# Third attention: the masks stored a second time with their halves exchanged, and added by 64-row, 64-column matmuls

## The reference, cut to what matters

```
def _L2_xattn_ref(queries, keys, values, masks, Wq, bq, Wk, bk, Wv, bv, Wo, bo):
    q = (queries @ Wq + bq).reshape(B, S, H, dk).transpose(0, 2, 1, 3)
    k = (keys @ Wk + bk).reshape(B, S, H, dk).transpose(0, 2, 1, 3)
    v = (values @ Wv + bv).reshape(B, S, H, dv).transpose(0, 2, 1, 3)
    scores = jnp.einsum('bhqd,bhkd->bhqk', q, k) / jnp.sqrt(jnp.float32(dk))
    scores = jnp.where(masks[:, None, :, :], scores, jnp.float32(-1000000000.0))
    attn = jax.nn.softmax(scores, axis=-1)
    out = jnp.einsum('bhqk,bhkd->bhqd', attn, v)
...
x = x + jnp.tanh(g_xattn[2]) * _L2_xattn_ref(_layernorm(x, axis=-1), ctx_1024, ctx_1024, mask_BxSxS2_bf1, ...)
```

## Time and profile before

| | us |
|---|---|
| median of three runs | 2752.37 |
| the three runs | 2749.81, 2752.37, 2772.16 |
| the profiled execution, its own time | 2753.38 |
| its span | 2751.6 |
| third attention in the span | about 1428 to 1880 |

### The profile page before, as it was taken

How to read it: one execution, slowest core, us unless ns; L and a number is a source line. 1 busy time by engine, 2 the same in 40 slices (tenths; PEclk the granted TensorE clock), 3 DMA queues, 4 the chain that set the end, 5 groups by cost and what they waited for, 6 DMA issues and landing times. The chain is left out here.

```text
span 2751.6 us, 77920 instructions
## 1 busy us (share of the span) xinstructions
PE 2249.3 (82%) x32227; PEld 1705.9 (62%) x32227; DVE 1791.9 (65%) x4725; ACT 1351.5 (49%) x2507; POOL 1217.9 (44%) x1731
## 2 busy tenths in 40 slices
PE   4999999999959599945648999983888848888597
PEld 3888888887747377734435766662555526666465
DVE  3777777777733488858866766644444458888544
ACT  2555555555513288829964544430111148777332
POOL 1333333434435411127751244445455566777535
PEclk9999999999979799976668988875899967677699
DMA  6112100000035211100000111111444322222263
GB/s 172 58 62 81 66 26 26 25 22 21 18 116 169 65 59 55 48 17 1 1 26 29 33 41 42 41 33 68 135 133 135 108 68 69 81 85 74 82 181 112
DMA packets 212353, 184.49 MB, mean 67 GB/s; under 512 B 33356, under 2 KB 187542, under 8 KB 212000
## 3 DMA queue, kind: packets, MB, share of 16 engines
q1 hardware_dynamic: 192544, 142.51, 17.6%
q0 software_dynamic: 19456, 36.99, 3.8%
HBM read 102.01 MB, written 72.68 MB: 63 GB/s over the span
## 5 line engine op out<-in xcount | busy, mean ns | idle before, releaser
L446 POOL DMA_INDIRECT slots<-row,put x256 | 264.4, 1033 | 251.0 <-issue 100.7
L1777 PE MATMUL experts_H<-experts_xs_t,experts_w 128*128 128x512 f32 x576 | 274.6, 622 | 26.5 <-DVE experts_xs_t L1702 22.3
L1649 POOL DMA_INDIRECT rows<-experts_y,experts_idx x160 | 155.4, 971 | 133.4 <-DVE experts_y L1726 88.1
L964 ACT ACTIVATE l_prob_t<-l_Z 128x512 f32<-128x512 f32 x256 | 132.2, 603 | 156.4 <-PE l_Z L1087 125.7
L1795 PE MATMUL experts_Y<-experts_w,experts_hid 128*128 128x128 f32 x1664 | 198.9, 276 | 10.3 <-DVE experts_y L1726 7.0
L1321 POOL TENSOR_TENSOR l_var_eps<-l_mv,eps 128x1 f32<-128x1 f32 x64 | 12.1, 189 | 430.9 <-DVE l_mv L1403 430.9
L1795 PEld LDWEIGHTS experts_Y<-experts_w,experts_hid 128*128 128x128 f32 x1664 | 192.4, 192 | 13.1 <-issue 13.1
L1777 PEld LDWEIGHTS experts_H<-experts_xs_t,experts_w 128*128 128x128 f32 x576 | 109.0, 200 | 142.1 <-issue 112.1
L878 DVE TENSOR_REDUCE l_top<-l_X 128x32 f32<-128x2048 f32 x64 | 146.6, 2290 | 72.8 <-PE l_X L1096 51.2
L1360 DVE TENSOR_REDUCE l_top<-l_S 128x16 f32<-128x1024 f32 x64 | 78.3, 1223 | 165.9 <-PE l_S L1499 165.9
L762 POOL TENSOR_TENSOR l_var_eps<-l_mv,eps 128x2 f32<-128x2 f32 x96 | 25.2, 262 | 333.1 <-DVE l_mv L860 228.2
(11 more groups left out here) (327 smaller groups left out, 5987.0 us busy)
## 6 DMA issues: line engine op xcount, KB each, us to landing
experts_w<-in_F_w SPq DMA_DIRECT2D x104, 256.0 KB
l_ctx_t<-in_ctx_t SPq DMA_DIRECT2D x96, 128.0 KB, 2.3
l_q_m<-l_q_t SPq DMA_DIRECT2D x384, 32.0 KB, 1.8
experts_xs<-slots SPq DMA_DIRECT2D x40, 264.0 KB
slots<-l_empty SPq DMA_DIRECT2D x16, 536.0 KB
experts_xs<-slots SPq DMA_DIRECT2D x16, 536.0 KB
slots<-l_empty SPq DMA_DIRECT2D x16, 520.0 KB, 5.1
experts_xs<-slots SPq DMA_DIRECT2D x16, 520.0 KB
```

The source lines that it names most:

```text
L446: pool.indirect_dma_start(self.slots, bass.IndirectOffsetOnAxis(ap=g.put[c][:, tile:tile + 1], axis=0), g.row[:, tile, self.sent_cols], No ...
L964: nc.scalar.activation(prob_t[:, t.par(PROB), r, :], Z[:, r, :], ACT.Exp).then_inc(prob_done, 1)
L1649: pool.indirect_dma_start(rows, bass.IndirectOffsetOnAxis(ap=idx[:, t.par(4, XS), k:k + 1], axis=0), y[:, t.par(4), k, :], None, bounds_ch ...
L1777: nc.tensor.matmul(H[:, c, :], w1_s[:, t.par(2), c, :], xs_t[:, t.par(2), :], start=True, stop=True).then_inc(h_filled[c], 1)
```

## The change

`hide` gets a further index of two: besides the mask with sequence 0 in partitions 0 to 63 and sequence 1 in 64 to 127, it holds the same with the two halves exchanged. The masks are laid out so in memory, so that the mask DMAs move twice the bytes. `mask_raw` is now a view of the memory of `prob_t`, which is written first two steps after the conversion. The matmuls of L1087 and L1096 become the function `hide_keys`: eight matmuls of 64 rows, 64 columns of weights and 512 moving columns (two tiles, four heads, 64 keys). For bank `r` and output half `b` the rows are half `b` where `r` is even and the other half where `r` is odd, so that four matmuls in a row use the four different quarters of the array.

```
-            mask_raw = ph.sb("mask_raw", [P, 2, TILES, 64], U8)
-            hide = ph.sb("hide", [P, 2, TILES, 64], BF16)
+            mask_raw = prob_t[:, :, :, :].rearrange("p a r n -> p (a r n)").bitcast(U8).rearrange("p (k h i n) -> p k h i n", k=2, h=2, n=64)
+            hide = ph.sb("hide", [P, 2, 2, TILES, 64], BF16)
...
-                    sp.dma_start(mask_raw[:, h, :, :], mask[h]).then_inc(weights_in, 16)
+                    sp.dma_start(mask_raw[:, h, :, :, :], mask[h]).then_inc(weights_in, 16)
...
-                    nc.gpsimd.tensor_scalar(hide[:, 1, :, :], mask_raw[:, 1, :, :], HIDE, -HIDE, ALU.mult, ALU.add).then_inc(hidden, 1)
+                    nc.gpsimd.tensor_scalar(hide[:, 1, :, :, :], mask_raw[:, 1, :, :, :], HIDE, -HIDE, ALU.mult, ALU.add).then_inc(hidden, 1)
...
-                    V.tensor_scalar(hide[:, 0, :, :], mask_raw[:, 0, :, :], HIDE, -HIDE, ALU.mult, ALU.add).then_inc(hidden, 1)
+                    V.tensor_scalar(hide[:, 0, :, :, :], mask_raw[:, 0, :, :, :], HIDE, -HIDE, ALU.mult, ALU.add).then_inc(hidden, 1)
...
+            def hide_keys(scores, kind, item):
+
+                for r in range(4):
+                    for b in range(2):
+                        half = 64 * (b ^ (r % 2))
+                        rows = slice(half, half + 64)
+                        last = nc.tensor.matmul(scores[64 * b:64 * b + 64, r, :], g.const_bf[rows, C_IDENT + half:C_IDENT + half + 64],
+                                                hide[rows, kind, r % 2, 2 * item:2 * item + 2, :].unsqueeze(2).broadcast_to([64, 2, 4, 64]),
+                                                start=False, stop=True)
+                return last
...
-                    for tile in range(2):
-                        for r in range(4):
-                            last = nc.tensor.matmul(Z[:, r, 256 * tile:256 * tile + 256], g.const_bf[:, C_IDENT:C_IDENT + P],
-                                                    hide[:, 1, 2 * t.item(PROB) + tile, :].unsqueeze(1).broadcast_to([P, 4, 64]),
-                                                    start=False, stop=tile == 1)
+                    last = hide_keys(Z, 1, t.item(PROB))
                     last.then_inc(p_filled, 1)
...
-                    for tile in range(2):
-                        for r in range(4):
-                            last = nc.tensor.matmul(X[:, r, 256 * tile:256 * tile + 256], g.const_bf[:, C_IDENT:C_IDENT + P],
-                                                    hide[:, 0, 2 * t.item(SCORE) + tile, :].unsqueeze(1).broadcast_to([P, 4, 64]),
-                                                    start=False, stop=tile == 1)
+                    last = hide_keys(X, 0, t.item(SCORE))
                     last.then_inc(s_filled, 1)
```

More of the change, by code:

```diff
@@ L2136, in lay_out @@
     m = a["mask_BxSxS2_bf1"].view(np.uint8)
-    o["mask"] = np.stack([x.reshape(TILES, P, SEQ).transpose(1, 0, 2) for x in (m, m.transpose(0, 2, 1))])
+    m = [x.reshape(TILES, 2, SEQ, SEQ) for x in (m, m.transpose(0, 2, 1))]
+    o["mask"] = np.stack([np.stack([y.reshape(TILES, P, SEQ).transpose(1, 0, 2) for y in (x, x[:, ::-1])], axis=1) for x in m])
     def halves(w):
```

## The result

The change makes the kernel slower by half a per cent: 2769.44 us median of 20 executions against 2756.79 us of 20 of the kernel before, ratio 1.0053, 95% interval 1.0034 to 1.0072. That is 13 to 15 us. Forecast was 2743 us with a range of 2727 to 2768; the time lies just above the range and on the other side of the kernel before. (An execution more than 1.5% above the fastest of its kernel is in the slow state and enters no ratio; one in all the experiments is.)

What follows compares the result with a forecast made beforehand. PE was taken to set the third attention's pace, with the mask additions on its loop. 2753.4 - 18 (steps) + 8 (start) = 2743.4 for an execution like the profiled one, 1.0 us above the median, so 2743 us; range 2727 to 2768.

Steps and rivals of the forecast that it cites:

- The additions are on PE's loop and fall from 0.89 to about 0.44 us: Third attention, L1087 and L1096: four quarters at once, 0.44 us to `Z`, 0.61 to `X`; PE gains 0.78 us a step.
- The analogy with L1201: L1201, 64 x 64 on four quarters, has the new load of 1024 units and takes 0.44 us without its tail.
- rival (a): Mask additions: row groups writing one bank collide, some 1.27 us an addition, about 2782 us, or 2767 if half collide; chance 0.12.
- L1109 is held by the exponential: L1109 needs L964's first exponential, so starts 1.33 us after the addition, not 1.05; 0.50 of 0.78 us remain.
- The start costs 8.2 us: Start of the third attention: 2.6 us mask DMA, 3.64 POOL's L785 holding up DVE, 2.0 DVE's L835.
- The sum over the steps, 18 us: Third attention: 30 steps at 0.50 us make 15.0, with -0.5, +2.6 and +1.0 for special steps; about 18 us off.
- rival (b): Third attention: less PE work brings more stretches at half clock, five to ten eat the gain, 2750 to 2762 us; chance 0.13.
- The step taken as typical, 10.25 us: Third attention, full clock: L1109 at 1552.67 to the next at 1562.92, 10.25 us, forecast to become 9.75.
- The prediction's own sign for the clock: Third attention: if the stage's granted clock falls below 0.8, the prediction is wrong and it is the clock.
- The argument against rival (b): The second attention, the same program without mask additions, ran at a granted clock of 1.00.

Runs made afterwards that it cites:

- the matmuls alone: Kernel before with only the four-at-a-time additions, both halves read from one stored copy, start unchanged: ratio 0.9976 (0.9950 to 1.0003), 6 us faster.
- the start alone: Kernel before with masks stored, moved and converted twice, additions unchanged: ratio 1.0027, 7 us slower; again on another chip 1.0030, 8 us slower.
- the last version: Against the kernel before: four-at-a-time additions, exchanged half copied within SBUF, addition to `Z` ahead of the scores to `X`: ratios 0.9952 and 0.9940.
- the lengthening: Kernel before with ten of 16 heads' products in L1145 issued again from step 13: ratio 1.0120, and 1.0164 on a chip with pauses.

## Why the prediction was wrong, step by step

*The additions are on PE's loop and fall from 0.89 to about 0.44 us.* Right: 0.46. The analogy with L1201, another group on four quarters, held. Of rival (a), that two row groups writing one bank get in each other's way, nothing is left in the time: two row halves write one bank at once here, and the group takes just what half of the full-array work takes (0.46 and 0.45 us). The rule quoted there from the Trainium skill, "TensorEngine Tiling (Array Packing)", Restrictions and Gotchas, doesn't show itself in time where the two tiles write different partitions of the bank.

*L1109 is held by the exponential.* Right: the wait of 0.36 us ahead of L1112 is in the trace, and L1112 comes 1.42 us after the addition where 1.33 was said. The gain of a full-clock step is 0.41 us instead of 0.50.

*The start costs 8.2 us.* 7.1 us in the profile (2.7 by the DMA, 3.4 by POOL holding up DVE, the rest by DVE's own conversion, for which 2.0 was said), and 7 to 8 us in two timed experiments. Slightly over-sized.

*The sum over the steps, 18 us.* This is the step that failed. It took the clock as unchanged and put rival (b) at 0.13. Even at full clock the sum would have been at most 31 x 0.41 = 13 us, and it counted one interval bound by DVE where its own trace has six. The half-clock time then rose with the short additions, in the whole execution by 22, 30 and 33 us (7 of the 33 by the start) on chips without pauses and by 35 and 62 on one with them, against 7 to 15 us for six series whose additions stream as long as before (the unchanged kernel among them) on chips without pauses. Where the narrow group was lengthened it rose with the old additions too, by 21 and 36. On the chips without pauses that left some 6 us in the matmuls alone, by an interval that reaches from 0 to 13, and nothing of the change after the start is paid. On the chip with pauses the steps took 379.0 and 375.1 us against 375.9 in place of 18 us less: some 7 us shorter at equal half-clock time, and 150 and 136 us of it instead of 113. The step taken as typical, 10.25 us, was a short one there too. Rival (b) had the mechanism, but with 2750 to 2762 us it was priced too low as well. The time lies only 1.4 us above the range, but the range reached that far for rival (a), bank sharing, at 2767, which didn't happen; that it nearly holds the time is luck. The prediction's own sign for the clock, below 0.8 in the stage, was just met in parts of it (0.77) and not in its mean (0.80). The argument against rival (b), that the second attention ran at a clock of 1.00 without any mask additions, was wrong: its steps of 7.4 us have no router work, and PE waits for nothing between its groups in that window, so it isn't the same case.

*The rest of the 13 to 18 us.* The start gives 7 of them, if it costs there what it costs on the other chips, and the steps nothing to speak of. In both profiles of the change on a chip with pauses the stages behind take some 11 us more (of them 6.5 in the fourth attention, 374.0 against 367.5 us, with 214 instead of 193 us of half clock), with the same code. But the fourth attention also took 372 us with the start alone, 375 with the last version and 362 with the change on a chip without pauses, and in one profile with pauses, the old additions and the lengthening, the stages behind were 8 us longer as well. Whether the change makes it slower there or these are the places where stretches at half clock happened to fall, isn't settled. Nor is why PE pauses on one kind of chip; the record only shows that the kernel before has the same first twelve intervals in this stage on both kinds, to 0.02 us, and differs from the thirteenth on (15.70 and 10.25 us).

## What to carry to other kernels

A saving on TensorE can be worth less than its length: here about half of some 12 us went back as half-clock time on chips without pauses, and all of it on the other. Where TensorE alternates between streaming and narrow groups, look at the granted clock of the stage before counting on a shorter streaming group, and try edits that also take away waits between the groups: of the versions with all masks, that with the copy in SBUF and the addition moved was the only one clearly faster than the kernel before, though its half clock rose as well (+38 and +39). And price the preparation of a second copy of the data at the start of the stage: made by DMA within SBUF behind other work it cost nothing (23.8 us to the first L878 against 24.5), converted again it cost 7 us of a gain of at most 13.

## What the runs showed of the hardware

- In this kernel PE's half-clock time went with the length of the mask additions and not, as far as can be told, with how much of the array they use: two 64 x 64 tiles at a time for 0.89 us had +11 us of half clock and the full array for 0.89 us +9, the full array for 0.45 us +30 and four tiles for 0.46 us +22. Each is uncertain by some 15 us; short against long, all series on chips without pauses together, it's 19 us, give or take 9. One profile with long additions (the addition to `Z` moved) goes against it.
- A us of half clock cost about a quarter to a third of a us: in the fourth attention, same code throughout, 362, 367, 374 and 375 us went with 171, 193, 214 and 225 us of half clock, about 0.25 us each; in the steps of the third it was 0.27 and 0.28, over whole executions of the unchanged kernel 0.28 to 0.36.
- Two 64-row matmuls from different row halves that write one PSUM bank in different partitions ran at once: the group took 0.46 us from start to start, half of the full-array work 0.45.
- A conversion on POOL held up a cast on DVE for its whole length: 3.64 and 3.70 us, 7.05 and 7.11 us, where a cast of the same size took 0.28 alone.
- Chips differed by 4% on this program, 2652 against 2756 us, and with it in what a change is worth: the change was at 1.0015 (0.9994 to 1.0037) on one and at 1.0065 (1.0042 to 1.0088) on another.
